# Reading gather indices in place instead of through a staging copy, in the expert and combine stages of a graph/mixture-of-experts kernel

## The reference, cut to what matters

```
xt   = layernorm(x)                                  # (6250, 256)
top_p, top_idx = top_k(softmax(xt @ Wr + br), 2)      # 2 of 8 experts for each node
weights = top_p / top_p.sum(-1)
xn   = (xt - mean) * rsqrt(var + eps)
h    = gelu((xn * ln_g[e] + ln_b[e]) @ W1[e] + b1[e]) # 256 -> 1024, per expert e
y    = h @ W2[e] + b2[e]                              # 1024 -> 256
out  = sum over the 2 chosen experts of weights * y
x    = x + out
```

## Time and profile before

| | us |
|---|---|
| timed runs: median (lowest to highest) | 7864.47 (7858.81 to 7873.66) |
| profiled execution, its own time | 7869.87 |
| its span (first to last instruction) | 7868.1 |
| expert stage, first gather to the barrier | 2679 to 3591 |
| combine stage, to the last normalised row | 3591 to 3745 |

### The profile page before, as it was taken

The page is one execution under the profiler, slowest core; times in us unless marked ns, Lnnn a source line. Parts: engine busy times, 40 slices in busy tenths (PEclk is TensorE's granted clock), DMA queues, the critical chain, the costliest instruction groups (busy, mean ns, idle before and its releaser), DMA issues. The chain is left out here.

```text
span 7868.1 us, 110058 instructions
## 1 busy us (share of the span) xinstructions
PE 5554.7 (71%) x27644; PEld 4678.6 (59%) x27645; DVE 3895.8 (50%) x10085; ACT 1587.9 (20%) x3574; POOL 5661.0 (72%) x6057
## 2 busy tenths in 40 slices
PE   3888888888883698992455555555555689999993
PEld 3666666666663588881344334333434589999983
DVE  4777777888888400004454444444444633333326
ACT  1222222222220333330000000000000234444441
POOL 3777777777776677776677777777777767777762
PEclk7888888888885799996777777777777879988886
DMA  3333333333334244444333333333332123333698
GB/s 120 105 105 105 106 105 102 98 97 96 97 96 124 97 155 153 154 155 116 110 105 97 93 93 92 93 92 93 92 93 81 26 71 81 79 80 78 76 71 184
DMA packets 428345, 799.53 MB, mean 102 GB/s; under 512 B 129927, under 2 KB 267899, under 8 KB 427982
## 3 DMA queue, kind: packets, MB, share of 16 engines
q0 software_dynamic: 237808, 481.17, 27.0%
q1 hardware_dynamic: 190430, 317.21, 12.0%
HBM read 726.97 MB, written 70.98 MB: 101 GB/s over the span
## 5 line engine op out<-in xcount | busy, mean ns | idle before, releaser
L1048 PE MATMUL g_pM<-g_G,g_S 128*128 128x256 f32 x3328 | 1219.3, 545 | 1264.4 <-DMA g_G<-table,g_IDX 1232.8
L746 POOL DMA_INDIRECT g_G<-table,g_STG x1664 | 1658.9, 997 | 478.3 <-issue 445.6
L760 POOL DMA_INDIRECT g_G<-table,g_IDX x1664 | 1584.6, 952 | 537.9 <-issue 506.0
L1048 PEld LDWEIGHTS g_pM<-g_G,g_S 128*128 128x128 f32 x3328 | 934.4, 288 | 1549.4 <-issue 1295.9
L1018 PE MATMUL g_pM<-g_G,g_S 128*128 128x260 f32 x3328 | 1122.6, 476 | 388.3 <-DVE acc L861 378.1
L601 POOL DMA_INDIRECT slots<-sort_PAIR,sort_ADDR x1024 | 1043.7, 1019 | 379.9 <-issue 310.9
L1591 POOL DMA_INDIRECT q_G<-table,slot x1072 | 1027.1, 958 | 362.2 <-issue 322.7
L869 DVE TENSOR_TENSOR acc<-g_pM,acc 128x256 f32 x1664 | 697.5, 419 | 1109.9 <-PE g_pM L1048 1107.0
L1018 PEld LDWEIGHTS g_pM<-g_G,g_S 128*128 128x128 f32 x3328 | 689.5, 227 | 677.1 <-DVE acc L861 562.0
L861 DVE TENSOR_TENSOR acc<-g_pM,acc 128x260 f32 x1664 | 710.6, 427 | 167.9 <-PE g_pM L1018 24.2
L849 DVE TENSOR_SCALAR g_S<-iota,g_REL,g_WT 128x128 f32<-128x128 f32 x1664 | 583.4, 351 | 189.7 <-issue 172.7
(11 more groups left out here) (322 smaller groups left out, 7264.5 us busy)
## 6 DMA issues: line engine op xcount, KB each, us to landing
e_W<-in_L_ffn_W SPq DMA_DIRECT2D x210, 512.0 KB
sort_PAIR<-slot_rows SPq DMA_DIRECT2D x66, 512.0 KB, 4.7
g_G<-table,g_STG POOLq DMA_INDIRECT x1664
g_G<-table,g_IDX POOLq DMA_INDIRECT x1664
ys_all<-ew_Y SPq DMA_DIRECT2D x196, 128.0 KB, 1.7
sm_Y<-ys_all SPq DMA_DIRECT2D x28, 896.0 KB
q_ST<-slot_rows SPq DMA_DIRECT2D x34, 512.0 KB, 3.9
sort_ADDR<-slot_rows SPq DMA_DIRECT2D x34, 512.0 KB
```

The costliest lines, as they stand in the source:

```text
L746: pool.indirect_dma_start(G[:, r, u, :], None, table, bass.IndirectOffsetOnAxis(ap=STG[:, r, u:u + 1].bitcast(U32), axis=0)).then_inc(gath ...
L760: pool.indirect_dma_start(G[:, r, u, :], None, table, bass.IndirectOffsetOnAxis(ap=IDX[:, k * GRP + u:k * GRP + u + 1].bitcast(U32), axis= ...
L1048: m = pe.matmul(pM[r % 2 * 2 + half][:, u % HG, :], S[:, r, u, :], G[:, r, u, :], start=True, stop=True)
```

## The change

In both stages the gathers read their row numbers directly from `node_of` and `pos_get`. The staging tiles, their copies, the semaphores `staged` and `slot_free`/`set_free`, and the waits for them are gone. Reading in place needs constant column numbers, so the POOL program of `combine` is written out instead of looped (that of `experts` was already). POOL's wait for the earlier gather of the same buffer goes too; the wait for `tin`, or for the sums of the round before last, stays. Separately, PE raises `h` twice a tile, after chunks 3 and 7, instead of eight times, and the three places that wait for it count accordingly.

```
-    s = {n: sh.sem(f"{tag}_{n}") for n in ("staged", "slot_free", "tin", "xt", "h", "gelu", "y", "yc")}
+    s = {n: sh.sem(f"{tag}_{n}") for n in ("tin", "xt", "h", "gelu", "y", "yc")}
...
-        STG = sc.sb(f"{tag}_STG", [P, 2], I32)
...
-                    sp.wait_ge(s["h"], t * HC)
+                    sp.wait_ge(s["h"], t * (HC // BC))
...
-            def fetch(rnd, j):
-                t, b = rnd * SLOTS + j, j % 2
-                at_least(pool, s_x[b], (rnd * (SLOTS // 2) + j // 2) * 16)
-                pool.tensor_copy(STG[:, b:b + 1], node_of[:, bass.ds(t, 1)]).then_inc(s["staged"], 1)
+            for t in range(NT):
                 at_least(pool, s["tin"], t - 1)
-                pool.wait_ge(s["staged"], t + 1)
-                pool.sem_inc(s["slot_free"], 1)
-                pool.indirect_dma_start(XI[:, b, :], None, rows, bass.IndirectOffsetOnAxis(
-                    ap=STG[:, b:b + 1].bitcast(U32), axis=0)).then_inc(s_x[b], 16)
-
-            if sort is None:
-                over_tiles(pool, fetch)
-            else:
-                for t in range(NT):
-                    fetch(t // SLOTS, t % SLOTS)
-                    sort.place(pool, count)
+                pool.indirect_dma_start(XI[:, t % 2, :], None, rows, bass.IndirectOffsetOnAxis(
+                    ap=node_of[:, t:t + 1].bitcast(U32), axis=0)).then_inc(s_x[t % 2], 16)
+                sort.place(pool, count)
...
-                at_least(a, s["h"], (t - 1) * HC)
+                at_least(a, s["h"], (t - 1) * (HC // BC))
...
-                        a.wait_ge(s["h"], t * HC + c + BC)
+                        a.wait_ge(s["h"], t * (HC // BC) + c // BC + 1)
...
-                    m.then_inc(s["h"], 1)
+                    if c % BC == BC - 1:
+                        m.then_inc(s["h"], 1)
...
-        STG = sc.sb(f"{tag}_STG", [P, 2, TOP, U7], I32)
...
-            def step(rnd, par):
-                it = rnd * 2 + par
-                at_least(pool, s_got[par], rnd * PAIRS * 16)
-                pool.tensor_copy(STG[:, par], pos_get[:, :, bass.ds(it * U7, U7)]).then_inc(s["staged"], 1)
+            for it in range(NB // U7):
+                par = it % 2
                 at_least(pool, s["sum"], (it - 1) * PAIRS)
-                pool.wait_ge(s["staged"], it + 1)
-                pool.sem_inc(s["set_free"], 1)
-                for u in range(U7):
+                for i in range(it * U7, (it + 1) * U7):
                     for k in range(TOP):
-                        pool.indirect_dma_start(R[:, par, k, u, :], None, ys, bass.IndirectOffsetOnAxis(
-                            ap=STG[:, par, k, u:u + 1].bitcast(U32), axis=0)).then_inc(s_got[par], 16)
-
-            every_pair(pool, step)
+                        pool.indirect_dma_start(R[:, par, k, i % U7, :], None, ys, bass.IndirectOffsetOnAxis(
+                            ap=pos_get[:, k, i:i + 1].bitcast(U32), axis=0)).then_inc(s_got[par], 16)
```

More of the change, by code:

```diff
@@ L2317, in combine @@
     nc = sh.nc
-    s = {n: sh.sem(f"{tag}_{n}") for n in ("staged", "sum", "set_free")}
+    s = {n: sh.sem(f"{tag}_{n}") for n in ("sum",)}
     s_got = [sh.lasting_sem(f"{tag}_got{j}") for j in range(2)]
```

## The result

| | us |
|---|---|
| changed kernel, timed runs: median (lowest to highest, 4 runs) | 7780.14 (7766.55 to 7784.31) |
| kernel before, in the same comparison (4 runs) | 7864.71 (7858.81 to 7873.66) |
| ratio, 95% interval | 0.9888 (0.9874 to 0.9901) |
| the same on a second chip (4 runs against 21) | 0.9883 (0.9868 to 0.9898) |
| profiled execution of the changed kernel, its span | 7783.16, 7781.4 |

The change takes 85 us off, 1.1%. It was predicted at 90 us (7775, range 7760 to 7800).

A forecast was written before the change was run, and what follows sets the result against it. POOL's chain was taken to bound the expert stage, PE close second. 1.0 + 72.8 + 12.5 - 2 + 5.4 = 89.7 us off the profiled 7869.87; taken from the median 7864.47 this gave 7775, range 7760 to 7800.

The forecast's parts named there:

- POOL is the bound of the expert stage: Expert stage: POOL runs its own chain at 8.41 us a tile without waiting; PE, needing 7.24, is the close second.
- 0.70 us a tile, 72.8 us: Expert stage: copy 0.20 and gap 0.80 go, a gap of 0.30 comes; 0.70 us less for each of 104 tiles.
- The five long gaps: Expert stage: five 3.29 us gaps between copy and gather go, 12.5 us gained; rival that they stay, 7787, chance 0.17.
- PE as the neighbour: Expert stage: PE keeps up with POOL's 7.71 us a tile but ends 2 us behind, bounds 0 and 8.
- the work behind the last turn: End of the expert stage: PE's work after its last turn is the same in both kernels, 0 us.
- The first gather behind a barrier: Start of both stages: the first gather loses copy and gap, 1.0 us in the expert stage, 1.05 in the combine stage.
- The later rounds of the combine stage: Combine stage: each of the six later rounds loses 0.72 us of copy and gap, 4.3 us in all.
- 98 combine gathers about 1.25 apart: Combine stage, sign of being right: gathers evenly about 1.25 us apart, with no break of 1.0 at each round.
- The signal: PE raising h less often: each wait is met by the same matmul, so 0, bounds 0 to 1 us gained.
- In-place reads: Rival, both stages: each in-place gather costs 1.00 us more by itself, giving 7989 us; chance 0.03.
- The gap did belong to the handshake: Rival, both stages, said the opposite: the 0.80 gap belongs to the gather and stays, only copies go, 7842; chance 0.03.
- PE did not become the bound: Rival, expert stage, said the opposite: PE becomes the bound at 7.86 us a tile, 7807; chance 0.12, wholly or half.

The follow-up runs named there:

- four_steps: Changed kernel with four expert sort steps a tile instead of five, the 105 left over issued behind its last gather; expert gathers 743.0 us first to last.
- copy_ahead: Kernel before, staging copies kept, but the copy for the next expert tile made between the third and fourth sort step; 7789.80 us, ratio 0.9903.
- more_code: Kernel before with four more semaphore increments per expert tile in POOL's program, which nothing waits for; one execution, 7866.77 us.
- moved_16: Changed kernel with 16 expert sort steps moved: ten behind the last expert gather, six behind the last combine gather; 0.9938 on the 9192 us chip, 0.9864 on a 7873 us chip.

## Why the prediction was right, point by point

*POOL is the bound of the expert stage: right.* Shortening POOL's chain alone gave the gain, and PE followed. PE's 7.24 is the floor, as read (four_steps).

*0.70 us a tile, 72.8 us: 0.73, 76.2 us.* The gather also fell from 1.01 to 0.99 us, inside the bounds. Right in sum, wrong in its parts: I gave the copy 0.20 and the handshake 0.50. It is 0.07 and 0.66 (copy_ahead), since the gap behind a copy is 0.16. For this change it did not matter; for someone who wants to keep the copy it does.

*The five long gaps, 12.5 us with 0 as the other bound: gone, 12.5.* The argument, that they stand only where POOL waits for itself, held in both kernels without the exposed wait (changed and copy_ahead). That a POOL which can run ahead covers them fits this, but no run shows it. That they go with the length of the program is refuted by more_code, and what they are stays open.
The Trainium skill ("Runtime: NRT & Kernel Launch", "Instruction fetch mechanics") has the crossing of a block border mostly hidden. More_code agrees as far as it goes: half as much program again moved none of the long gaps. Of the rule itself the runs show no more than that, and it said nothing on whether the gaps would go.

*PE as the neighbour, 2 us lost at the end: 1.9 gained.* PE's last matmul ended 21.5 us behind the last gather before and 19.6 now. The forecast put the work behind the last turn at the same in both kernels. It is not: PE's last wait before, of 2.00 us, was followed by a stretched group, which now takes 3.72 instead of 5.40. The two PE groups behind the last turn and at the stage's end, before and then after:

```profile
3571.68 5.40 PE L2292 MATMUL e_pY<-ew_W,e_GT 128*128 x16 [0.31 <-issue]
3584.82 3.72 PE L2292 MATMUL e_pY<-ew_W,e_GT 128*128 x16 [0.71 <-DVE e_Y L2262]
```

```profile
3482.90 3.72 PE L2281 MATMUL e_pY<-ew_W,e_GT 128*128 x16 [0.26 <-issue]
3494.35 3.72 PE L2281 MATMUL e_pY<-ew_W,e_GT 128*128 x16 [0.71 <-DVE e_Y L2250]
3501.53 0.99 POOL L2364 DMA_INDIRECT c_R<-ys,pos_get  x1 [15.69 <-PEq L118]
```

PE waited 7 times instead of 42, and the clock stayed up (0.99). By the earlier trace rows the old waits were themselves what cost PE 0.6 to 1.5 a tile.

*The first gather behind a barrier, 1.0 us in the expert and 1.05 in the combine stage: 0.4 each.* The forecast let the gather start where the copy had stood. It starts 0.7 us later than that. In the expert stage POOL sat idle 7.52 us ahead of the copy, and sits idle 8.18 ahead of the gather (before, then after):

```profile
2678.67 0.19 POOL L2202 COPY e_STG<-node_of 128x1 int32<-128x1 int32 x1 [7.52 <-POOLq L118]
```

```profile
2679.71 0.99 POOL L2200 DMA_INDIRECT e_XI<-rows,node_of  x1 [8.18 <-POOLq L118]
```

The gain does not show in the table, since the stage ahead ended 0.4 us later in that profile. In the combine stage the first gather started 3.83 us behind PE's last matmul before (3588.54 to 3592.37 in the earlier trace rows) and starts 3.46 behind it now.

*The later rounds of the combine stage, 4.3 us: 5.3.* The copies and gaps gave 4.3 as forecast; the other 1.0 is the gathers' own issue time, 102.1 before and 101.1 now, which differs by more than that from profile to profile. The sign "98 combine gathers about 1.25 apart" did not come in full, since some take up to 2.47 to issue. Behind the last gather 1.0 was given back in this pair; in the second profile of the changed kernel 0.2 was. *The signal, 0: 0.*

*The sum.* The parts measured in the pair of profiles are 0.4 + 76.2 + 12.5 + 1.9 + 0.4 + 5.3 - 1.0 = 95.7 us, where 89.7 was forecast: the mechanism was right, the tile 0.03 us too small, PE's end on the wrong side and the two starts too large. The medians show 84.6, and on the second chip 94.8. So that the first comparison came within 5 us of the forecast is partly luck. Where its missing 10 us are is not shown, since only one execution of each kernel was profiled there; in that pair the slot pass took 14.7 back, the kernel before having the shortest of all profiles.

*The rivals.* In-place reads do not cost more (0.988 to 0.992 us each). The gap did belong to the handshake. PE did not become the bound.

## What to carry to other kernels

An engine that issues indirect DMAs back to back, with 0.30 us behind each as here, is at its limit even at a busy share of 70%; add up its chain, gaps included, before looking at which engine is busiest. In such a chain a wait for the engine's own last instruction costs far more than the instruction: make the copy a few instructions early (0.07 us a tile here, against 0.73), or read in place. And once such a chain is shorter, measure the next engine's floor by taking work off it, and see what ends the stage behind it: steps moved into idle time are free only up to the point where they end the stage themselves.

## What the runs showed of the hardware that was not expected

About every 102nd indirect DMA on POOL, from the 217th of the stage on, is followed by a stall that adds 2.49 us, but at the usual speed only where the gather behind it waits for a copy that POOL has just made; in the kernels without an exposed wait it does not show. Four more semaphore increments a tile on POOL cost nothing measurable. The gap behind a copy on POOL before an indirect DMA that does not wait for it was 0.16 us, against 0.30 behind an indirect DMA. Behind a barrier an indirect DMA started 0.7 us later than a copy did (idle 8.18 against 7.52). One of the chips ran the kernel before in 9192 us instead of 7870, with a granted clock of 0.75 (0.69 in one of eleven executions) instead of 0.79 to 0.80; in the expert stage POOL started 3.15 us after the PE instruction it waited for, instead of 0.28, and a gain in POOL's chain (moved_16, 0.9864) shrank there to 0.9938.
